# Moving the six key parts of each stacked half from the sync engine's DMA queue to POOL's own

## The chip, the cores and the metric

The kernel runs on one core of a Trainium2 chip. The metric is the time of one execution on the device, in microseconds (us); three runs of the kernel before gave 576.96 us as their median (576.51 to 578.29).

## The reference, cut to what matters

One transformer layer over x of shape (4, 512, 256), in float32: cross attention with 16 heads of 16 columns, then a mixture of experts (8 experts, top 2, plus a shared one). The change lies in the attention, where the queries come from the normalised x, the keys and values from the first 512 rows of a context (the causal mask leaves no later row), and the scores are Q K^T / 4:

```python
Q = (query @ Wq.T + bq).reshape(B, Sq, H, dk).transpose(0, 2, 1, 3)
K = (key @ Wk.T + bk).reshape(B, Sk, H, dk).transpose(0, 2, 1, 3)
scores = jnp.einsum('bhqd,bhkd->bhqk', Q, K) / jnp.sqrt(jnp.float32(dk))
scores = jnp.where(causal, scores, -jnp.inf)
attn = jax.nn.softmax(scores, axis=-1)
out = jnp.einsum('bhqk,bhkd->bhqd', attn, V)
```

## The kernel before

**Halves and stacks.** A batch of x has 512 rows and 16 heads; eight heads make a half, so there are 8 halves over the four batches. The float32 queries and keys of a half are split into three bf16 parts each (`parts`, 128 partitions by 512 columns a part). Since a head has only 16 columns, six products of parts are summed by one matmul of 96 rows: the six strips of 16 partitions of `qstack` hold the query parts in the order `Q_PART`, those of `kstack` the key parts in the order `K_PART`. Each strip is filled by one DMA that reads a part from all 128 partitions and writes 16 partitions, 1 KB a piece, 128 KB in all. So a half costs 12 such DMAs. `stack(half, u)` (L352 to L358) issues them on the sync engine SP, first the six of the queries, then the six of the keys, and all 12 count on the semaphore `rows_in[half]`.

**Who makes the parts.** TensorE (PE) projects (L643), DVE adds the bias and writes `val` (L1142), ACT rounds part 1 and part 2 (L940), and the remainders between (L502) and part 3 (L507) are POOL's in the loop, DVE's (L1149, L1154) for the first two halves. Two of the halves (u = 0 and 1) are made ahead of the loop, and each of the loop's three turns makes two more: half 0 of the next batch in the second slot, half 1 in the fourth.

**The slots.** A batch has four groups of four heads. `slot(g, ...)` on PE interleaves, by the list `SLOT`, the row maxima's scores of the next group ("R", L592 and L594, into `set_a`), the product with V of the group before ("PV", L622), and the transposed scores of this group ("S", L612, into `set_b`, which ACT's exponential L987 empties). Slots 1 and 3 begin with a projection for a coming half. The "R" matmuls of slot 3 are the first that read the new half 0, those of the next turn's slot 1 the first that read the new half 1; ahead of them stands `pe.wait_ge` on `rows_in` (L684). ACT waits for the same semaphore before it writes part 1 of the next half (L952), since the stack's DMAs read `parts`.

**The masks.** POOL sets the diagonal blocks of the exponentials to zero (L521), one call for each k of 0 to 3 in a group; `probs_v` on PE waits for `p_masked` of its k before each PV. The PVs of a group are made in the next slot: k = 0 and 1 near its start, k = 2 and 3 after "S" 7 (one row of 16 matmuls in the trace). In `mask_group` (L510 to L522) of slots 1 and 3, POOL makes part 3 between mask k = 1 and mask k = 2.

**The row maxima's rows.** `max_rows` (L361 to L364) is a DMA of 12 KB that SP issues from the same queue; the first "S" of a slot waits for it. SP works in the order of its program: in each turn `max_rows(2)`, a DMA of zeros to `x_by_slot`, `stack(0)`, `max_rows(3)`, two of zeros, `max_rows(0)`, zeros, `stack(1)`, `max_rows(1)`.

**Before the loop.** SP issues `stack(0, 0)`, `stack(1, 1)`, then `max_rows(0)`. POOL, after its constants, waits for the normalised x of all batches and adds the bias of the output to x (L489, 8.82 us).

Of the kernel before, what the change touches and what calls it, by code (L numbers as in the profile page):

```python
# [41 lines left out]
DMA = 16  # L42


def build(nc, x, ctxT, wqT, bq, wkT, bk, wvT, bv, woT, bo, gwT, wupT, wdnT, sgT, suT, sdT, out):
    B, S, D = x.shape
    H = NUM_HEADS
    DK = D // H
# [18 lines left out]
    Q_PART = (0, 0, 1, 1, 0, 2)  # L67
    K_PART = (0, 1, 0, 1, 2, 0)
# [3 lines left out]
    with ExitStack() as ctx:  # L72
# [3 lines left out]
        def sem(name):  # L76
            return ctx.enter_context(nc.semaphore(name))
# [155 lines left out]
        rows_in = [sem("rows_in0"), sem("rows_in1")]  # L233
# [4 lines left out]

        a_full, a_free, b_full, b_free = sem("a_full"), sem("a_free"), sem("b_full"), sem("b_free")
        p_masked, rc_ready, pool_turns = sem("p_masked"), sem("rc_ready"), sem("pool_turns")  # L240

        lt_full, lt_read, lg_read, logits_full, route, d_ready, ex_ready, sel_ready = (sem(n) for n in
            ("lt_full", "lt_read", "lg_read", "logits_full", "route", "d_ready", "ex_ready", "sel_ready"))
# [39 lines left out]
        B_SLOT = S_N + 1  # L283
# [43 lines left out]
        def _(sp):  # L327
# [23 lines left out]

            def stack(half, u):  # L352

                for a, (dst, order) in enumerate(((qstack, Q_PART), (kstack, K_PART))):
                    sp.wait_ge(parts_ready, 2 * u + a + 1)
                    for j, part_of in enumerate(order):
                        sp.dma_start(dst[DK * j:DK * (j + 1), half, :, :],  # L357
                                     parts[:, a, part_of, :]).then_inc(rows_in[half], DMA)  # L358

            def max_rows(g, n):  # L360
                sp.wait_ge(b_free, n + 1)  # L361
# [14 lines left out]
            def batch(b, final):  # L376
                n_b = B_ATT + b * B_PER
                if not final:

                    sp.wait_ge(a_full, A_PRO + b * A_PER - 1)  # L380
                    sp.dma_start(cV, ctxT[bass.ds(b + 1, 1)].rearrange("o (c p) n -> p (o c) n", p=P)[:, :, 0:S]
                                 ).then_inc(ld_cv, DMA)
                max_rows(2, n_b + MAX_AT)
                if not final:
                    zero_rows(4 * b + 1)
                    sp.wait_ge(b_full, n_b + B_SLOT)
                    stack(0, 2 * b + 2)
                max_rows(3, n_b + B_SLOT + MAX_AT)
                if final:
                    for w, w_dram in ((wsg, sgT), (wsu, suT), (wsd, sdT), (gw, gwT)):  # L390
                        sp.dma_start(w[:], w_dram.rearrange("(c p) n -> p c n", p=P)).then_inc(ld_moe, DMA)
                else:
                    zero_rows(4 * b + 2)
                    zero_rows(4 * b + 3)
                    max_rows(0, n_b + 2 * B_SLOT + MAX_AT)
                    zero_rows(4 * b + 4)
                    sp.wait_ge(b_full, n_b + 3 * B_SLOT)
                    stack(1, 2 * b + 3)
                    max_rows(1, n_b + 3 * B_SLOT + MAX_AT)
                    sp.dma_start(wdn[:, bass.ds(b, 1), :], wdnT[bass.ds(b * P, P)].rearrange("p (o n) -> p o n", o=1)  # L400
                                 ).then_inc(ld_moe, DMA)
# [52 lines left out]
        def _(pool):  # L454
# [29 lines left out]
            g.memset(credit[:, 0:1], 0.0).then_inc(s_yfree, 1)  # L484
            g.memset(credit[:, 1:2], 0.0).then_inc(e_yr, 1)

            pool.wait_ge(ld_o, DMA * 2)
            pool.wait_ge(xs_ready, B)
            g.tensor_tensor(xs_all[:], xs_all[:],  # L489
                            bo_bc.rearrange("p (o d) -> p o d", o=1).to_broadcast([P, T, D]),  # L490
                            ALU.add).then_inc(bo_added, 1)


            def pool_turn(signal, count):

                pool.wait_ge(signal, count)
                pool.sem_inc(pool_turns)

            def remainders(u):
                for a in range(2):  # L500
# [6 lines left out]
                    g.tensor_tensor(parts[:, a, 2, :], rem[:, a, :], parts[:, a, 1, :],  # L507
                                    ALU.subtract).then_inc(parts_ready, 1)

            def mask_group(n, last=False, split=None):  # L510

                if split is not None:
                    remainders(split)
                for k in range(QT):
                    if k == 2 and split is not None:
                        part3(split)

                    jobs = sum(job[0] <= k for job in S_JOBS)
                    pool_turn(b_free, n + jobs + (1 if jobs > MAX_AT and not last else 0))
                    diag = pT[k][:, :, 0:P]  # L520
                    g.affine_select(out=diag, in_=diag, compare_op=ALU.is_ge, fill=0.0, base=0,  # L521
                                    pattern=[[0, HG], [1, P]], channel_multiplier=-1).then_inc(p_masked, 1)  # L522

            mask_group(B_GRP0)
            with pool.Fori(0, B - 1) as b:
                for s in range(NG):
                    mask_group(B_ATT + b * B_PER + s * B_SLOT, split={0: 2 * b + 2, 2: 2 * b + 3}.get(s))
            for s in range(NG - 1):
                mask_group(B_ATT + (B - 1) * B_PER + s * B_SLOT, last=s == NG - 2)

# [42 lines left out]
        def _(pe):  # L573
# [85 lines left out]
            project_v(2, 2, 0, cT)  # L659
            pe.wait_ge(consts, 4)  # L660
            pe.wait_ge(fills, 3)
            pe.wait_ge(rows_in[0], DMA * 12)
            for j in range(A_GRP):
                rowmax_scores(0, j, 3 + j, 3 + j)
            maxima(MAX_0, B + 2, 1, first=True)
# [8 lines left out]
            def slot(g, count, n_b, par_b, rows=None, projection=None, wait_rows=None,  # L674
                     pv=True):

                at = 0
                if projection:  # L680
                    projection(*rows)
                    at = 1
                if wait_rows:
                    pe.wait_ge(*wait_rows)  # L684
                for kind, j in SLOT:
                    if kind == "R" and rows:
                        rowmax_scores((g + 1) % NG, j, rows[0] + at + j, rows[1] + at + j)
                    elif kind == "PV" and pv:
                        probs_v((g - 1) % NG, count - 1, j)
                    elif kind == "S":  # L690
                        if j == 0:
                            pe.wait_ge(max_in, DMA * (count + 1))
                        skip = 1 if rows and j >= MAX_AT else 0
                        scoresT(g, j, n_b + j + skip, par_b + j + skip)
                    elif kind == "MAX" and rows:
                        maxima(n_b + MAX_AT, par_b + MAX_AT, count + 2)
# [36 lines left out]
            def batch(b, final):  # L733
# [10 lines left out]

                for g in range(1, NG):

                    wait_rows = ((rows_in[1], DMA * 12 * (b + 1)) if g == 1 else
                                 (rows_in[0], DMA * 12 * (b + 2)) if g == 3 and not final else None)
                    projection = next_half(g // 2) if g != 2 else None
                    rows = None if final and g == 3 else (n_a, par_a)  # L750
                    slot(g, count + g, n_b, par_b, rows, projection, wait_rows)
                    if rows is not None:
                        jobs = A_GRP + (projection is not None)
                        n_a, par_a = n_a + jobs, par_a + jobs
                        n_b, par_b = n_b + 1, par_b + 1
                    n_b, par_b = n_b + S_N, par_b + S_N
# [182 lines left out]
        def _(act):  # L939
# [9 lines left out]
            def part1(u, n, w):  # L949

                if w is not None:
                    act.wait_ge(*w)  # L952
                for a in range(2):
                    act.wait_ge(*((val_ready, u + 1), (a_free, n + 1))[a])
                    copy(parts[:, a, 0, :], val[:, a, :]).then_inc(part1_ready, 1)
# [11 lines left out]
            part1(0, 0, None)  # L967
            part2(0)
            deviations(1, QT, T)
            part1(1, 1, (rows_in[0], DMA * 12))  # L970
            part2(1)

            def max_rows(n, par):
# [30 lines left out]
            def batch(b, final):  # L1004
                n, par = B_ATT + b * B_PER, B_ATT
                n_a = A_PRO + b * A_PER
                count = b * NG
                for g in range(1, NG):
                    u = None
                    if g != 2 and not final:  # L1010
                        u, job = (2 * b + 2, n_a) if g == 1 else (2 * b + 3, n_a + 2 * A_GRP + 1)

                        part1(u, job, (rows_in[1], DMA * 12 * (b + 1)) if g == 1 else
                              (rows_in[0], DMA * 12 * (b + 2)))
                    n, par = exps(n, par, (g - 1, count + g - 1), not (final and g == NG - 1), u)
                if final:
                    deviations(2, 0, T - QT)
                    p_v(NG - 1, count + NG - 1)
                    ln2_copies(0)
                    ln2_copies(1)  # L1020
                    n, par = n + 2 * C, par + 2 * C
                else:
                    n, par = exps(n, par, (NG - 1, count + NG - 1))
                for tiles in A_TILES:
                    act.wait_ge(b_full, n + 1)
                    w = len(tiles) * P
                    copy(attnT.rearrange("p c n -> p (c n)")[:, tiles[0] * P:tiles[0] * P + w],
                         bank(par)[:, 0:w]).then_inc(b_free, 1)
                    n, par = n + 1, par + 1
# [428 lines left out]
```

## Time and profile before

| what | us |
|---|---|
| median of three runs | 576.96 |
| span of the profiled execution | 575.3 |
| PE busy | 482.2 |
| DVE busy | 287.6 |
| ACT busy | 204.3 |
| POOL busy | 161.4 |
| DMA wait on the chain that ended last, `attention` to `attention` | 7.1% of the span |

The profile lists one execution with the times of each engine's instructions. The span is the time from its first to its last instruction. "SPq" and "POOLq" are instructions on an engine's own queue, DMA issues above all. A name like `attention<-attention` gives the tensor written and the tensor read; all buffers of the attention stage lie in one tensor called `attention`. In brackets at the end of a row of the timeline stands the engine's idle time ahead of it and what ended it. PEclk is the TensorE clock that was granted, as a share of 2.4 GHz; 0.50 is 1.2 GHz.

### The profile page before, as it was taken

How to read it: one execution, taken by the hardware profiler on the slowest of the kernel's cores; microseconds unless marked ns; L12 is line 12 of the kernel's file. 1: busy time of each engine (PE TensorE's matmuls, PEld its weight loads, DVE VectorE, ACT ScalarE, POOL GpSimd, SP SyncE). 2: the span in 40 equal slices, each digit the busy share in tenths (PEclk: the TensorE clock that was granted, in tenths of full speed). 3: DMA queues.
4: the chain of work that ended last, by engine and by line, in shares of the span. 5: the costliest groups of instructions: out<-in, count | busy, mean ns of one | idle time of the engine just before them, and what ended most of it. 6: DMA issues, size and time to landing. Idle time of an engine off the chain costs nothing.

```text
span 575.3 us, 9801 instructions
## 1 busy us (share of the span) xinstructions
PE 482.2 (84%) x2849; PEld 312.9 (54%) x2850; DVE 287.6 (50%) x590; ACT 204.3 (36%) x415; POOL 161.4 (28%) x186
## 2 busy tenths in 40 slices
PE   4536896999978997998879999279999999999890
PEld 2314442474424642473353555268888888888650
DVE  6746373647555572646544666114343433434357
ACT  1213464544536163544663444013232323232110
POOL 7004342312324043311211287601222222221200
PEclk9957799999979998998999999779999999999995
DMA  8759229191837539290207422212222222221168
GB/s 267 171 54 112 65 54 144 39 174 38 122 72 111 137 65 129 53 159 2 83 3 291 173 86 93 98 40 64 57 66 62 65 64 64 64 64 55 37 191 255
DMA packets 48193, 56.66 MB, mean 98 GB/s; under 512 B 10640, under 2 KB 43472, under 8 KB 47536
## 3 DMA queue, kind: packets, MB, share of 16 engines
q1 hardware_dynamic: 44768, 47.10, 38.0%
q0 software_dynamic: 3408, 9.34, 4.5%
q8 instruction: 10, 0.16, 0.1%
q14 instruction: 7, 0.06, 0.0%
HBM read 27.05 MB, written 16.59 MB: 76 GB/s over the span
## 4 chain that ended last, share of the span: by engine, by line
PE 53%; DMA 12%; DVE 9%; issue 7%; ACT 7%; POOL 6%; SPq 5%; ACTq 0%; POOLq 0%; DVEq 0%
PE set_b L889 9%; DMA attention<-attention 7%; POOL x_by_slot L555 6%; PE set_a L873 6%; PE set_a L592 5%; PE set_a L875 5%; PE set_a L874 5%; PE set_b L622 5%; SPq L357 5%; ACT attention L987 4%; PE set_a L643 3%; PE set_b L612 3%; DVE attention L1190 3%; PE set_a L798 2%; PE set_b L881 2%
## 5 line engine op out<-in xcount | busy, mean ns | idle before, releaser
L1190 DVE TENSOR_REDUCE attention<-set_a 128x2 f32<-128x1024 f32 (+2 forms) x96 | 96.7, 1042 | 57.5 <-PE set_a L594 55.6
L987 ACT ACTIVATE attention<-set_b 128x512 f32<-128x512 f32 (+1 forms) x176 | 87.5, 565 | 69.4 <-PE set_b L612 68.7
L592 PE MATMUL set_a<-attention 96*128 96x512 bf16 (+3 forms) x256 | 67.8, 330 | 32.7 <-DMA attention<-attention 26.0
L564 POOL DMA_INDIRECT y_by_choice<-moe,e_dst x39 | 37.2, 955 | 140.4 <-DVE moe L1372 131.8
L521 POOL TENSOR_SCALAR_AFFINE_SELECT attention<-attention 128x512 f32<-128x512 f32 x64 | 39.8, 634 | 116.3 <-ACT attention L987 116.2
L592 PEld LDWEIGHTS set_a<-attention 96*128 96x128 bf16 x256 | 26.7, 104 | 80.1 <-issue 46.2
L612 PE MATMUL set_b<-attention 99*128 99x512 bf16 (+3 forms) x256 | 60.8, 312 | 11.0 <-ACT attention L987 6.0
L1358 DVE TENSOR_TENSOR moe<-set_a,moe 128x384 f32<-128x384 f32 x39 | 21.7, 557 | 92.0 <-ACT moe L1075 92.0
L889 PE MATMUL set_b<-w_down,moe 128*128 x234 | 60.3, 388 | 1.1 <-DVE moe L1372 1.1
L1075 ACT ACTIVATE moe<-set_a 128x384 f32<-128x384 f32 x39 | 19.1, 490 | 116.7 <-PE set_a L875 116.7
L873 PE MATMUL set_a<-wup_hi,e_xT_hi 128*128 x156 | 57.1, 366 | 1.6 <-DVE e_xT_lo L1353 1.2
L594 PE MATMUL set_a<-maskb,identb 128*128 128x128 bf16 x256 | 53.4, 236 | 0.0
L875 PE MATMUL set_a<-wup_hi,e_xT_lo 128*128 x156 | 53.3, 341 | 0.0
L874 PE MATMUL set_a<-wup_lo,e_xT_hi 128*128 x156 | 53.1, 340 | 0.0
L622 PE MATMUL set_b<-attention 128*32 128x128 f32 (+3 forms) x512 | 47.3, 470 | 0.8 <-ACT attention L940 0.7
L889 PEld LDWEIGHTS set_b<-w_down,moe 128*128 128x128 f32 x234 | 40.0, 190 | 10.3 <-issue 7.2
L555 POOL DMA_INDIRECT x_by_slot<-moe,slots x32 | 35.1, 1098 | 28.2 <-DVE slots L1335 18.7
L643 PE MATMUL set_a<-attention 128*128 (+1 forms) x64 | 31.9, 644 | 9.0 <-DMA attention<-in_ctxT 7.8
L612 PEld LDWEIGHTS set_b<-attention 99*128 99x128 bf16 x256 | 19.6, 99 | 34.3 <-ACT attention L987 20.6
L940 ACT ACTIVATE attention<-attention 128x512 bf16<-128x512 f32 x32 | 19.3, 644 | 52.6 <-DMA attention<-attention 26.6
L873 PEld LDWEIGHTS set_a<-wup_hi,e_xT_hi 128*128 128x128 f32 x156 | 29.9, 192 | 11.1 <-issue 10.2
L940 ACT ACTIVATE attention<-set_b 12x512 bf16<-12x512 f32 (+4 forms) x48 | 25.7, 594 | 25.0 <-PE set_b L786 13.2
(152 smaller groups left out, 691.3 us busy)
## 6 DMA issues: line engine op xcount, KB each, us to landing
attention<-attention SPq DMA_DIRECT2D x96, 128.0 KB, 5.7
wup<-in_wupT SPq DMA_DIRECT2D x2, 3072.0 KB, 14.1
x_by_slot<-attention SPq DMA_DIRECT2D x13, 387.0 KB, 7.4
moe<-x_by_slot SPq DMA_DIRECT2D x39, 128.0 KB, 2.0
moe<-y_by_choice SPq DMA_DIRECT2D x16, 256.0 KB, 3.8
attention<-in_ctxT SPq DMA_DIRECT2D x7, 512.0 KB, 5.9
w_down<-in_wdnT SPq DMA_DIRECT2D x3, 1024.0 KB, 8.6
x_res<-in_x SPq DMA_DIRECT2D x4, 512.0 KB, 7.2
```

The source lines that it names most:

```text
L555: g.indirect_dma_start(xg, bass.IndirectOffsetOnAxis(slots[:, k, t:t + 1], 0), xn2[:, t, :], None).then_inc(scattered, DMA)
L592: mm(dst, qstack[0:ROWS, g // 2, h, k * P:w], kstack[0:ROWS, g // 2, h, 0:w], start=True, stop=False)
L594: last = mm(dst[:, k * P:w], identb[:], maskb[:], start=False, stop=True)
L612: last = mm(bank(par)[:, i * w:(i + 1) * w], kstack[0:ROWS + 3, g // 2, h, k * P:(k + 1) * P], qstack[0:ROWS + 3, g // 2, h, k * P:S], sta ...
L622: last = mm(pv_bank[32 * h:32 * h + 32, k * P:S], vaug[:, k, HG * g + h, :], pT[k][:, h, :], start=k == 0, stop=k == QT - 1, tile_position ...
L643: last = mm(pair(A, par)[:, a, :], w[:, c, half * P:(half + 1) * P], src[:, c, bass.ds(b * S, S)], start=c == 0, stop=c == C - 1)
L873: mm(dst, e_xT_hi[:, a, c, :], wup_hi[:, c, cols], start=c == 0, stop=False)
L874: mm(dst, e_xT_hi[:, a, c, :], wup_lo[:, c, cols], start=False, stop=False)
L875: last = mm(dst, e_xT_lo[:, a, c, :], wup_hi[:, c, cols], start=False, stop=c == C - 1)
L889: last = mm(Bk[:, 2, 0:D], e_hT[:, a, m, :], wdn[:, m, bass.ds(e * D, D)], start=m == 0, stop=m == M - 1)
L987: nc.scalar.activation(pT[k][:, h:h + heads, :], bank(par)[:, 0:heads * (S - k * P)], ACT.Exp).then_inc(b_free, 1)
L1190: v.tensor_reduce(dst, src, AX.X, ALU.max, negate=True).then_inc(a_free, 1)
```

## The change

The keys' six DMAs of a half leave SP. POOL issues them, in the same order of strips, on its own queue, and they count on new semaphores `keys_in[half]`. Where PE and ACT waited for 12 landings on `rows_in`, they wait for six on `rows_in` and six on `keys_in`. In the loop, POOL's `stack_keys` stands between part 3 and mask k = 2; it waits for `keys_read`, which SP raises once its own wait for the end of the slot's matmuls has passed. Ahead of the loop POOL issues the keys of the first two halves before it adds the output's bias.

```diff
             def stack(half, u):
-                for a, (dst, order) in enumerate(((qstack, Q_PART), (kstack, K_PART))):
-                    sp.wait_ge(parts_ready, 2 * u + a + 1)
-                    for j, part_of in enumerate(order):
-                        sp.dma_start(dst[DK * j:DK * (j + 1), half, :, :],
-                                     parts[:, a, part_of, :]).then_inc(rows_in[half], DMA)
+                sp.wait_ge(parts_ready, 2 * u + 1)
+                for j, part_of in enumerate(Q_PART):
+                    sp.dma_start(qstack[DK * j:DK * (j + 1), half, :, :],
+                                 parts[:, 0, part_of, :]).then_inc(rows_in[half], DMA)
...
                     sp.wait_ge(b_full, n_b + B_SLOT)
+                    sp.sem_inc(keys_read)
                     stack(0, 2 * b + 2)
...
                     sp.wait_ge(b_full, n_b + 3 * B_SLOT)
+                    sp.sem_inc(keys_read)
                     stack(1, 2 * b + 3)
...
+            def stack_keys(u, half):
+                pool_turn(parts_ready, 2 * u + 2)
+                for j, part_of in enumerate(K_PART):
+                    g.dma_start(kstack[DK * j:DK * (j + 1), half, :, :],
+                                parts[:, 1, part_of, :]).then_inc(keys_in[half], DMA)
+
+            stack_keys(0, 0)
+            stack_keys(1, 1)
             pool.wait_ge(ld_o, DMA * 2)
...
-            def mask_group(n, last=False, split=None):
+            def mask_group(n, last=False, split=None, half=None):
...
                     if k == 2 and split is not None:
                         part3(split)
+                        pool_turn(keys_read, split - 1)
+                        stack_keys(split, half)
...
-            pe.wait_ge(rows_in[0], DMA * 12)
+            pe.wait_ge(rows_in[0], DMA * 6)
+            pe.wait_ge(keys_in[0], DMA * 6)
...
                 if wait_rows:
-                    pe.wait_ge(*wait_rows)
+                    half, count_in = wait_rows
+                    pe.wait_ge(rows_in[half], count_in)
+                    pe.wait_ge(keys_in[half], count_in)
...
                 if w is not None:
-                    act.wait_ge(*w)
+                    half, count_in = w
+                    act.wait_ge(rows_in[half], count_in)
+                    act.wait_ge(keys_in[half], count_in)
```

## Rows read from the trace of the kernel before

**Rows 1.** The page: the chain that ended last, by engine.
```profile
PE 53%; DMA 12%; DVE 9%; issue 7%; ACT 7%; POOL 6%; SPq 5%; ACTq 0%; POOLq 0%; DVEq 0%
```

**Rows 2.** Waits: engine, line, releaser: us in total, times, longest.
```profile
ACT attention L940 <- DMA attention<-attention: 26.6, 4, 8.1
PE set_a L592 <- DMA attention<-attention: 26.0, 4, 13.6
```

**Rows 3.** Timeline of PE: start, us, instruction, idle before.
```profile
36.97 0.59 PE L592 MATMUL set_a<-attention 96*128 96x512 bf16 x1 [13.55 <-DMA attention<-attention]
...
59.13 0.61 PE L612 MATMUL set_b<-attention 99*128 99x512 bf16 x1 [2.69 <-DMA attention<-attention]
...
98.30 0.47 PE L592 MATMUL set_a<-attention 96*128 96x512 bf16 x1 [4.17 <-DMA attention<-attention]
```

**Rows 4.** Timeline of SP's queue: start, us, instruction.
```profile
21.72 30.13 SPq L357 DMA_DIRECT2D attention<-attention  x24
51.89 0.86 SPq L363 DMA_DIRECT2D attention<-attention  x1
...
83.04 7.80 SPq L357 DMA_DIRECT2D attention<-attention  x12
...
112.40 8.46 SPq L357 DMA_DIRECT2D attention<-attention  x12
```

**Rows 5.** The issues of L357: ns each min/median/max, and landings.
```profile
L357 SPq DMA_DIRECT2D attention<-attention x96: 547/607/1326, 21.7 to 248.3; - x96
...
DMA to landing us min/median/max: 3.2/5.7/8.1
```

**Rows 6.** Timeline ahead of the loop: DVE's part 3, ACT's copy of the maxima's rows.
```profile
21.00 1.35 DVE L1154 TENSOR_TENSOR attention<-attention 128x512 bf16<-128x512 f32 x2
...
47.98 0.59 ACT L940 ACTIVATE attention<-set_b 12x512 bf16<-12x512 f32 x1 [5.52 <-PE set_b L602]
```

**Rows 7.** Windows: length, busy by engine, PEclk, DMA share, GB/s.
```profile
30.00:34.00 4.00, 0.00 (x0) 0.00 (x0) 0.37 (x2) 0.00 (x0) 0.00 (x0) 0.50 1.14 119
...
90.00:94.00 4.00, 3.95 (x14) 1.63 (x12) 0.00 (x0) 2.08 (x5) 1.56 (x3) 1.00 1.14 121
128.00:130.00 2.00, 2.00 (x11) 1.77 (x10) 0.42 (x1) 0.00 (x0) 0.00 (x0) 1.00 0.97 390
...
57.50:64.30 6.80, 5.17 (x26) 3.28 (x27) 2.70 (x4) 2.28 (x4) 3.03 (x2) 0.50 0.26 58
...
98.50:101.90 3.40, 3.40 (x15) 0.85 (x14) 1.23 (x1) 0.93 (x2) 2.26 (x2) 0.50 0.36 107
```

**Rows 8.** The chain in order of time: start, us, what.
```profile
28.92 7.80 DMA attention<-attention
...
90.23 7.95 DMA attention<-attention
```

**Rows 9.** Timeline of POOL, masks and part 3 of the loop's first turn.
```profile
79.69 2.27 POOL L507 TENSOR_TENSOR attention<-attention 128x512 bf16<-128x512 f32 x2
81.96 1.22 POOL L521 TENSOR_SCALAR_AFFINE_SELECT attention<-attention 128x512 f32<-128x512 f32 x2
```

**Rows 10.** Timeline of PE: the PVs of k = 2 and 3, the projection.
```profile
88.37 0.86 PE L622 MATMUL set_b<-attention 128*32 128x256 f32 x16
...
90.48 3.65 PE L643 MATMUL set_a<-attention 128*128 x8
...
117.79 0.86 PE L622 MATMUL set_b<-attention 128*32 128x256 f32 x16
```

**Rows 11.** Timeline of POOL: its indirect DMAs of the routing stage.
```profile
332.85 0.96 POOL L555 DMA_INDIRECT x_by_slot<-moe,slots  x1 [0.30 <-issue]
334.11 2.41 POOL L555 DMA_INDIRECT x_by_slot<-moe,slots  x1 [0.30 <-issue]
336.82 1.36 POOL L555 DMA_INDIRECT x_by_slot<-moe,slots  x1 [0.30 <-issue]
```

**Rows 12.** Timeline of DVE, beside those DMAs.
```profile
333.94 6.75 DVE L1348 TENSOR_TENSOR wup_lo<-wup,wup_hi 128x1536 fp32r<-128x1536 f32 x4
```

More of the change, by code:

```diff
@@ L240, in build @@
         p_masked, rc_ready, pool_turns = sem("p_masked"), sem("rc_ready"), sem("pool_turns")
+        keys_read = sem("keys_read")
+        keys_in = [sem("keys_in0"), sem("keys_in1")]
         lt_full, lt_read, lg_read, logits_full, route, d_ready, ex_ready, sel_ready = (sem(n) for n in
@@ L485, in _, with pool_turn @@
             g.memset(credit[:, 1:2], 0.0).then_inc(e_yr, 1)
+            def pool_turn(signal, count):
+                pool.wait_ge(signal, count)
+                pool.sem_inc(pool_turns)
+            def stack_keys(u, half):
[5 more added lines that the diff above has]
+            stack_keys(1, 1)
             pool.wait_ge(ld_o, DMA * 2)
@@ L491, in _ @@
                             ALU.add).then_inc(bo_added, 1)
-            def pool_turn(signal, count):
-                pool.wait_ge(signal, count)
-                pool.sem_inc(pool_turns)
             def remainders(u):
@@ L526, in _ @@
                 for s in range(NG):
-                    mask_group(B_ATT + b * B_PER + s * B_SLOT, split={0: 2 * b + 2, 2: 2 * b + 3}.get(s))
+                    mask_group(B_ATT + b * B_PER + s * B_SLOT, split={0: 2 * b + 2, 2: 2 * b + 3}.get(s),
+                               half={0: 0, 2: 1}.get(s))
             for s in range(NG - 1):
@@ L745, in batch @@
                 for g in range(1, NG):
-                    wait_rows = ((rows_in[1], DMA * 12 * (b + 1)) if g == 1 else
-                                 (rows_in[0], DMA * 12 * (b + 2)) if g == 3 and not final else None)
+                    wait_rows = ((1, DMA * 6 * (b + 1)) if g == 1 else
+                                 (0, DMA * 6 * (b + 2)) if g == 3 and not final else None)
                     projection = next_half(g // 2) if g != 2 else None
@@ L969, in _ @@
             deviations(1, QT, T)
-            part1(1, 1, (rows_in[0], DMA * 12))
+            part1(1, 1, (0, DMA * 6))
             part2(1)
@@ L1011, in batch @@
                         u, job = (2 * b + 2, n_a) if g == 1 else (2 * b + 3, n_a + 2 * A_GRP + 1)
-                        part1(u, job, (rows_in[1], DMA * 12 * (b + 1)) if g == 1 else
-                              (rows_in[0], DMA * 12 * (b + 2)))
+                        part1(u, job, (1, DMA * 6 * (b + 1)) if g == 1 else
+                              (0, DMA * 6 * (b + 2)))
                     n, par = exps(n, par, (g - 1, count + g - 1), not (final and g == NG - 1), u)
```

## The prediction, made before the changed kernel was run

> **What bounds the kernel now.** Read the page first: PE is busy for 482.2 of 575.3 us, and it has 53% of the chain that ended last, but DMA has 12% of it and SP's queue 5% [rows 1]. So not all of the time is PE's work. The waits name the DMAs: ACT and PE stood for 26 us each for transfers within `attention`, four times each [rows 2]; those are the stacks. The timeline of PE places them: 13.55 us ahead of the first "R", then 4.17 us at the "R" of slot 3 in the loop's first turn, and 4.20 and 4.06 us at the same place of the other two turns; beside these, 2.69 us ahead of the first "S" [rows 3]. The first four have the stack's landing as their end, the fifth the landing of `max_rows(0)`, which SP issued right behind 24 DMAs of two stacks [rows 4]. The chain goes the same way: last DMA of a stack issued at 28.92 and at 90.23, landed 7.8 and 7.95 us later [rows 8].
>
> Next comes why the rows land late, since that decides everything. SP issues 12 in 7.80 us, 0.65 us each [rows 4]. A DMA needs at the least 3.2 us from issue to landing, but the median is 5.7 [rows 5]: they queue. While they do, the queues are busy throughout (share 1.14) and move 119 to 121 GB/s [rows 7], so 131,072 bytes take 1.09 us, more than SP's 0.65 us. Twelve take 13.1 us. SP's issue is not what limits the stack; the movement of the data is. Yet the same 16 engines at a share of 0.97 move 390 GB/s when 2 KB pieces go to all partitions [rows 7]. What differs is that a stack's DMA writes 16 partitions only. Two DMAs in flight to different strips could thus go faster than two to one strip.
>
> **The change, part by part.** Six issues leave SP, 3.9 us a half; nothing on the chain waits for SP's own time but `max_rows(0)`. The new semaphores and waits of PE and ACT add an instruction each on queues that stand idle or run ahead there; I count nothing for them (a wait that is already met costs below 0.1 us, and even 20 of them on the path would be 2 us, which the range holds). What counts is two prices: how fast the rows land when two queues feed the engines, and what six issues cost POOL.
>
> *POOL's pace p.* No row of before shows a direct DMA from POOL. Below stands SP's pace for the same DMA, 0.65 us [rows 4]. The nearest row is POOL's indirect DMA, also 128 pieces of 1 KB: 0.96 us busy and 0.30 us to the next, a pace of 1.27 [rows 11]. Above stand the ones beside DVE's L1348, which reads two SBUF tensors: 1.36 busy, so 1.67, and one of 2.41 [rows 11, 12]. In the loop DVE mostly reduces out of `set_a` meanwhile, so I don't take the stretched ones. A direct DMA reads no list of indices, so I go a little under the nearest row: p = 1.2, of which 0.9 busy.
>
> *Landing.* I take it that the two queues mix: SP runs ahead by a strip at once (0.65 against 1.2 us), so that mostly two different strips are being written. The last key DMA then lands 3.2 us after its issue. It costs nothing if so, 0 to 5 us at each stop if not (the rival below).
>
> *Ahead of the loop.* Key part 3 is ready at 21.00 + 1.35 = 22.35 [rows 6], POOL is idle. Last key DMA issued 22.4 + 5p = 28.4, landed 31.6, in place of 36.7 [rows 8]: 5.1 us. In general 36.7 - 25.6 - 5p = 11.1 - 5p. The 2.69 us ahead of the first "S" go too: ACT's copy ends at 48.57 [rows 6], 43.5 when all is 5.1 earlier; SP is then through with its six (the second stack's twelve issues end at 51.85 [rows 4] and so began at 44.1; 44.1 - 5.1 + 3.9 = 42.9), so `max_rows(0)` goes out behind 6 stack DMAs and not 12, at 43.5, and PE asks for it at 56.4 - 5.1 = 51.3, 7.8 us later, as long as it needed before. Sum: 13.8 - 5p = 7.8 us. POOL's bias addition may start up to a microsecond later behind the keys of u = 1; nothing on the chain waits for it.
>
> *In the loop, slot 3.* POOL's part 3 ends at 81.96, then it waits with SP for `keys_read`; SP's stack starts at 83.04 [rows 4, 9]. Behind the six issues on POOL stand mask k = 2 and k = 3, which ran at 81.96 to 83.18 before. Issues end 6p - 0.3 = 6.9 later, mask k = 2 takes 0.63: 90.57. PE wants that PV at 88.37 [rows 10], and mask k = 3 costs it 0.17 more. So a new stop s = 6p - 0.3 + 0.63 + 0.17 - 5.33 = 6p - 4.83 = 2.4 us. This was hidden by 5.2 us of cover before, and now that is used up. PE reaches the "R" of slot 3 at 94.13 + 2.4 = 96.5. The keys land at 83.0 + 6.0 + 3.2 = 92.2, so no wait is left there: the mean stop of 4.1 us becomes 2.4.
>
> *Slot 4 (slot 0 of the next batch).* The same six issues come for half 1 at 112.40, the PV is wanted at 117.79, 5.39 later [rows 4, 10]: again 2.4 us. Here nothing is won: the rows are first read in the next turn's slot 1, behind the end of the batch. ACT and PE have no slack left by which to catch up after a PV, for the transposes of the output wait on it.
>
> *The clock.* After each 4.1 us stop PE ran at a granted clock of 0.50 for 3.4 us or more [rows 7]; at 1.2 GHz in place of 2.4 that is 1.7 us a turn. The stop of 2.69 us was followed by 0.50 too, 57.5 to 64.3. Two stops of 2.4 us in a turn in place of one of 4.1 may leave one such stretch, none or two. I take one: no change, with 1.7 us a turn to both sides.
>
> *Sum.* Ahead of the loop 13.8 - 5p, in the loop 3 (4.1 - 2s) = 3 (13.8 - 12p), together 55 - 41p: each 0.1 us of POOL's pace is worth 4 us. With p = 1.2 that is 7.8 - 2.0 = 5.8, rounded to 6 us faster. The profiled span is 575.3 us, so 569.3, and the median of the runs stands 1.7 us above it: 571.
>
> The Trainium skill, "SBUF — State Buffer", section "Door 1: The DMA port swizzle", says that partitions reach the DMA side over 16 ports, picked by bits of the partition number, so that a strip of 16 partitions has four. An estimate by its 27 GB/s a port is 109 GB/s for a strip, near the 119 to 121 measured, and by it two strips at a time would reach about twice that. By that rule the sum above stands.
>
> **The rivals.** *The data still bind.* The rows land as late as before whoever issues them: 120 GB/s, 13.1 us for twelve. For it speaks that the queues are at 1.14 already and SP has 5 us of lead; if POOL's j-th DMA moves in step with SP's j-th, both write one strip. Against it: 390 GB/s in another pattern. Then nothing is won ahead of the loop and in slot 3, where the 2.4 us are hidden before the unchanged 98.3, and slot 4 pays 3 x 2.4 = 7.1 us: 584 us. It decides where the twelve take D: x = 13.1 - D is won once ahead of the loop and in each of three turns, 4x against 7.1, so from x below 1.8, D above 11.3 us. The Trainium skill, "DMA: Bandwidth & Descriptors", section "Issuing engines are not separate DMA queues", says that issuing from several engines saves only the time on the sequencer; no run here has tested it yet, and by it this is the case that comes.
>
> *POOL's issues are dear.* At p = 1.5 the masks come 4.2 us late in two places of each turn: 13.8 - 7.5 = 6.3 won ahead, 3 (4.1 - 8.3) = -12.7 in the loop, 583 us. It turns slower from p = 1.34 on. The row of 1.27 lies near, those of 1.67 beyond.
>
> *POOL's issues are cheap.* At p = 0.95, s is 0.9: 9.1 + 3 (4.1 - 1.7) = 16 us, and stops of 0.9 us should leave the clock up, 3 x 1.7 = 5 more: 556 us. For it speaks the lack of indices; against it that both kinds write as many pieces.
>
> *It doesn't do what it says:* the new stop in slot 3 is as long as the old and the rows were never last. The named releaser of four stops speaks against that.
>
> **How the numbers follow.** The forecast 0.45 (p from 1.05 to 1.34, 565 to 577 us), data bind 0.22, dear issues 0.13, cheap issues 0.15, the rest 0.05. By the bounds of p: at 0.65 no stop is left, 10.5 + 12.3 + 5.1 gives 549; at 1.67, 5.4 - 18.6 gives 590. Leaving out the outer ends of the cheap and dear cases, 559 to 585. What can be told from no change here is 0.3%, 1.7 us. Faster: 0.38 of the forecast's share, the cheap case and a little of the rest, 0.56; same 0.10; slower 0.34.
>
> **What would show it.** POOL's issues in the profile: pace 1.2, six in 7 us. PE's first "R" near 31.8 in place of 36.97 and no wait for a DMA ahead of the first "S". In the loop, no DMA wait at L592, but two stops of about 2.4 us a turn at L622, released by POOL L521. During the stacks, well over 120 GB/s. The prediction is wrong if L592 still waits for `attention<-attention` in the loop, or if the PVs of k = 2 don't wait for the masks, or wait for over 4 us.

## The result, and the profile after

The changed kernel takes 582.11 us (median; 581.51 to 583.16) against 576.74 us of the kernel before: a ratio of 1.0085, 95% interval 1.0063 to 1.0108. It is 5.4 us slower; 6 us faster was forecast. The profiled execution has a span of 580.4 us against 575.3.

Waits of the changed kernel, which answer to [rows 2]:

```profile
ACT attention L957 <- DMA attention<-attention: 28.0, 4, 8.3
PE set_a L606 <- DMA attention<-attention: 27.4, 4, 13.8
```

None of the stops that were to go has gone. The timeline of PE, against [rows 3], says so at each place:

```profile
37.24 0.59 PE L606 MATMUL set_a<-attention 96*128 96x512 bf16 x1 [13.77 <-DMA attention<-attention]
...
59.87 0.61 PE L626 MATMUL set_b<-attention 99*128 99x512 bf16 x1 [3.17 <-DMA attention<-attention]
...
99.50 0.61 PE L606 MATMUL set_a<-attention 96*128 96x512 bf16 x1 [4.95 <-DMA attention<-attention]
```

The stops are 13.77, 3.17 and 4.95 us where they were 13.55, 2.69 and 4.17. The POOL rows, which answer to [rows 9], show what I had feared, the masks behind POOL's issues:

```profile
80.41 2.28 POOL L518 TENSOR_TENSOR attention<-attention 128x512 bf16<-128x512 f32 x2 [0.27 <-ACT attention L957]
84.07 3.14 POOL L499 DMA_DIRECT2D attention<-attention  x6 [1.39 <-SPq L388]
87.22 1.81 POOL L534 TENSOR_SCALAR_AFFINE_SELECT attention<-attention 128x512 f32<-128x512 f32 x3
```

POOL issues six DMAs in 3.14 us, a pace of 0.52 us, less than SP's 0.65 [rows 4] and less than half of the 1.2 that I took. The masks of k = 2 and 3 are through in time and the PV is not stopped:

```profile
88.79 0.64 PE L636 MATMUL set_b<-attention 128*32 128x256 f32 x8
```

Now the data. First come the window 90 to 94 us, the same as in [rows 7], and the stretch behind the stop (length, busy by engine, PEclk, DMA share, GB/s). Then follow the chain, and the landings of SP's and of POOL's stack DMAs:

```profile
90.00:94.00 4.00, 3.95 (x18) 1.84 (x16) 0.00 (x0) 2.49 (x5) 1.63 (x3) 1.00 1.05 108
98.50:105.20 6.70, 5.70 (x25) 1.23 (x26) 2.45 (x2) 1.15 (x2) 2.27 (x2) 0.50 0.37 107
```
```profile
87.00 12.38 DMA attention<-attention
```
```profile
L358 SPq DMA_DIRECT2D attention<-attention x48: 547/613/2298, 21.8 to 248.1; - x48
...
DMA to landing us min/median/max: 3.3/8.2/12.4
```
```profile
L499 POOL DMA_DIRECT2D attention<-attention x48: 530/530/760, 23.1 to 247.4; - x48
...
DMA to landing us min/median/max: 4.2/8.1/12.5
```

With two queues 108 GB/s are moved where one queue moved 121. The last of the twelve goes out at 87.00 us, 3.2 us before that of the old kernel (90.23 [rows 8]), and all that they do is wait longer: a median of 8.2 us to landing and not 5.7 [rows 5]. The last to land is that last query DMA of SP, 12.38 us after its issue. From the first issue to the last landing a stack takes 15.8 us in the first turn's slot 3, 15.4 and 15.0 in the others, where it took 15.1, 15.1 and 15.0, and 16.4 against 15.1 for the second stack ahead of the loop. The granted clock after the stop of 4.95 us is 0.50 for 6.7 us and not for 3.4 [rows 7].

By place: at the same matmul after the loop, which waits for DVE in all kernels, the changed kernel stands 3.1 us behind. The kernel before, then the changed one:

```profile
263.51 0.34 PE L592 MATMUL set_a<-attention 96*128 96x384 bf16 x1 [1.12 <-DVE attention L1190]
```
```profile
266.61 0.34 PE L606 MATMUL set_a<-attention 96*128 96x384 bf16 x1 [1.12 <-DVE attention L1209]
```

The span ends 5.1 us behind. So 2 us are lost after the attention, where the change touches nothing. The routing stage's indirect DMAs on POOL, which answer to [rows 11], before and then after:

```profile
L555 POOL DMA_INDIRECT x_by_slot<-moe,slots x32: 956/960/2406, 326.4 to 370.0; - x32
```
```profile
L569 POOL DMA_INDIRECT x_by_slot<-moe,slots x32: 965/969/2522, 329.0 to 373.9; - x32
```

From the start of the first to the end of the last they take 45.94 us against 44.59, which is 1.35 of the 2 us. The rest comes behind them, where kernels differ by as much without the change: from the end of these DMAs to the end of the span pass 205.5 us here and 204.3 before, and 204.2 to 205.4 in the five other kernels below in which POOL issues no direct DMA.

### The profile page after: what moved, and what is told of

The parts are those of the page before. It is cut to its first block, busy times and chain, and to the rows that moved or that the text cites. A ratio compares the mean times of both kernels' runs of the same rounds, so it can differ in the third digit from the quotient of the medians.

```text
span 580.4 us, 9830 instructions
## 1 busy us (share of the span) xinstructions
PE 484.7 (84%) x2849; PEld 312.4 (54%) x2850; DVE 288.0 (50%) x590; ACT 204.2 (35%) x415; POOL 188.5 (32%) x234
## 4 chain that ended last, share of the span: by engine, by line
PE 53%; DMA 16%; DVE 9%; POOL 7%; issue 6%; ACT 6%; SPq 3%; ACTq 0%; POOLq 0%; DVEq 0%
DMA attention<-attention 10%; PE set_b L906 9%; POOL x_by_slot L569 6%; PE set_a L890 6%; PE set_b L636 5%; PE set_a L606 5%; PE set_a L892 5%; PE set_a L891 5%; ACT attention L1006 4%; PE set_a L657 3%; DVE attention L1209 3%; PE set_a L815 2%; PE set_b L626 2%; DMA moe<-y_by_choice 2%; PE set_b L898 2%
## 5 line engine op out<-in xcount | busy, mean ns | idle before, releaser
L636 PE MATMUL set_b<-attention 128*32 128x128 f32 (+3 forms) x512 | 50.8, 501 | 0.4 <-ACT attention L957 0.3
L569 POOL DMA_INDIRECT x_by_slot<-moe,slots x32 | 36.5, 1140 | 28.2 <-DVE slots L1354 18.7
L499 POOL DMA_DIRECT2D attention<-attention x48 | 25.6, 541 | 39.4 <-DVE attention L1173 29.8
```

The source lines that it names most:

```text
L569: g.indirect_dma_start(xg, bass.IndirectOffsetOnAxis(slots[:, k, t:t + 1], 0), xn2[:, t, :], None).then_inc(scattered, DMA)
L636: last = mm(pv_bank[32 * h:32 * h + 32, k * P:S], vaug[:, k, HG * g + h, :], pT[k][:, h, :], start=k == 0, stop=k == QT - 1, tile_position ...
```

## The experiments

Theory A says that the write into 16 neighbouring partitions binds a stack's DMAs, theory B that an engine moves such pieces at that rate wherever they go. The rows of a stack may stand in any order, so long as queries and keys have the same; that makes A easy to test. The kernel before, spread:

```diff
-                        sp.dma_start(dst[DK * j:DK * (j + 1), half, :, :],
+                        sp.dma_start(dst[j:ROWS:6, half, :, :],
```

> The kernel before, with the 96 rows of the stacks laid out otherwise: part j of column d goes to partition 6d + j in place of 16j + d, for queries and keys alike, so that the sums are the same and each DMA writes 16 partitions that lie 6 apart. Theory A (the write into 16 neighbouring partitions binds a stack at 1.09 us a DMA): the twelve run at SP's pace of 0.65 us, the rows land near 32 us in place of 36.7 ahead of the loop, the stops of 4.1 us in the loop go with their stretches of half clock, 5.8 us a turn; 552 us. Theory B (an engine moves pieces from SBUF to SBUF at about 7.5 GB/s whatever they write): nothing changes, 577 us.

Measured: 548.80 us, ratio 0.9501 (0.9473 to 0.9529), and once more 548.50, 0.9499 (0.9477 to 0.9522). Its repetition had this expectation:

> The spread kernel before once more, on the chip of the kernel with ACT's six DMAs, to compare the two: 549 us, as the first time.

The waits, the window of a stack in the second turn, and the landings of the spread kernel:

```profile
PE set_a L592 <- DMA attention<-attention: 8.7, 1, 8.7
...
ACT attention L940 <- DMA attention<-attention: 3.2, 1, 3.2
```
```profile
134.00:140.00 6.00, 5.58 (x56) 3.13 (x55) 4.26 (x8) 4.86 (x11) 1.27 (x2) 1.00 0.75 208
```
```profile
DMA to landing us min/median/max: 2.3/2.4/3.7
```

The three stops in the loop and that ahead of the first "S" are gone; the one ahead of the first "R" is left, with 8.7 us. The queues move 208 GB/s at a share of 0.75, and no DMA waits for another: 2.4 us from issue to landing is the median as well as nearly the least. Theory A holds and B falls: only the place of the 16 partitions was changed. Here SP's issue is what binds.

The changed kernel in the same layout (`qstack[j:ROWS:6, ...]` on SP, `kstack[j:ROWS:6, ...]` on POOL):

> The changed kernel with the same layout of rows, partition 6d + j. Theory A: with the write unbound, the two queues' issues count (SP 0.65, POOL 0.52 us each, side by side), rows land near 29 us ahead of the loop, some 3 us before those of the kernel before in this layout; in the loop both are early enough; 549 to 552 us. Theory B: 582 us, as the changed kernel.

Measured: 550.58 us, 0.9533 (0.9509 to 0.9557). The stop ahead of the first "R" is 8.06 in place of 8.66 us, and that is all that the second queue gains: the last of the twelve is issued 4.2 us after the first, where SP by itself needs 7.2, but they still land 0.65 us apart. In the profiles it stands 0.4 us behind the spread kernel on one queue after the loop and 3.8 at the end, so again the loss comes after the attention: 1.4 us of it are in the 32 indirect DMAs (45.98 against 44.59). The medians are 1.8 us apart.

The keys' strips from the last to the first in the changed kernel:

```diff
-                for j, part_of in enumerate(K_PART):
+                for j, part_of in reversed(list(enumerate(K_PART))):
```

> The changed kernel; POOL issues the keys' strips from the sixth to the first while SP goes from the first to the sixth, so the two queues write different strips nearly always. If the two queues of the changed kernel only met in the same strip, this frees them: over 150 GB/s during a stack, rows 3 us or more earlier, 570 us or less. If all 16 engines take their turns between the queues in step, so that they are all in one strip at any time whatever the order, or if theory B holds: about 120 GB/s and 582 us.

Measured: 576.58 us, 0.996 (0.993 to 0.999), midway between the two forecasts. Waits and first "R" of slot 3:

```profile
PE set_a L606 <- DMA attention<-attention: 25.0, 4, 13.5
```
```profile
97.13 0.41 PE L606 MATMUL set_a<-attention 96*128 96x512 bf16 x1 [3.87 <-DMA attention<-attention]
```

From first issue to last landing a stack of slot 3 takes 14.6 to 14.8 us, where the old kernel took 15.0 to 15.1 and the changed one 15.0 to 15.8. The matmul after the loop is at 262.09 us, 4.5 us ahead of the changed kernel and 1.4 ahead of the old one (0.4 us of that stood already when its first stack was issued). Only the order of the strips differs from the changed kernel, and the two intervals of the ratio (0.993 to 0.999, 1.0063 to 1.0108) lie apart, so the order costs the changed kernel time. The reading is that its two queues meet in the same strip: POOL's first issue comes 0.5 us behind SP's, and its fifth is ahead of SP's fifth. But two strips at once don't give twice the rate; a stack is through 2 to 3% sooner than with one queue.

The packets of the traces show more. POOL's are of 4 KB and SP's of 1 KB, so they can be told apart, and their order gives the strip. Of the time in which both queues have a packet under way, both write the same strip for 37% in the changed kernel and for 5% in this one. And of the time in which both have a stack to write, one queue holds 90% or more of the packets under way for 40% here: with some 16 packets under way at a time, the engines swing together from one queue to the other. But while neither holds over 70% (23% of the time), the packets move at 139 GB/s, and at 124 while one holds nearly all. So even side by side, two strips are not written at twice the rate.

All twelve on POOL (the query loop moved into `stack_keys`):

> The changed kernel with all twelve DMAs of a half issued by POOL, queries then keys, on its one queue. If it is the alternation between two queues that makes the stack of the changed kernel last 14.5 us and not 13.7: first packet to last landing is back near 13.5 us, the stops at the first row maxima of slot 3 are 4.2 us, and what is added are the masks behind six more issues (3.1 us), a stop of 1 to 2 us before the PV of k = 2 in slots 3 and 4: 579 to 584 us. If it is POOL's descriptors themselves (4 KB packets): the twelve take 15 us or more, and the time is over 585 us.

Measured: 581.46 us, 1.0068 (1.0046 to 1.0091). The twelve take 14.7 to 14.8 us from first issue to last landing in the loop (15.4 in one stack of six; the old kernel 15.0 to 15.3), so POOL's descriptors are no slower than SP's. The masks behind twelve issues:

```profile
87.82 1.01 PE L636 MATMUL set_b<-attention 128*32 128x256 f32 x16 [2.21 <-POOL attention L534]
```
```profile
80.83 3.15 POOL L496 DMA_DIRECT2D attention<-attention  x6 [1.70 <-SPq L385]
83.97 3.15 POOL L499 DMA_DIRECT2D attention<-attention  x6
87.12 2.39 POOL L534 TENSOR_SCALAR_AFFINE_SELECT attention<-attention 128x512 f32<-128x512 f32 x4
```

This is the stop that the prediction had put into the changed kernel, at 12 x 0.52 in place of 6 x 1.2: issues end at 87.12, a mask takes 0.63, PE goes on at 87.82. It comes at all six places, with 2.1 to 2.2 us each. PE wanted the PV at 85.61, 4.8 us after POOL's first issue and not the 5.33 of the prediction; six issues at 0.52 us fit under either.

Two layouts between neighbours and stride 6. The kernel before at stride 3:

```diff
+                        sp.dma_start(dst[48 * (j // 3) + j % 3:48 * (j // 3) + 48:3, half, :, :],
```

> The kernel before with each DMA of a stack writing 16 partitions that lie 3 apart (part j of column d at 48 (j // 3) + j % 3 + 3d). If the 16 partitions' sharing of ports binds, by the port table of the Trainium skill up to three of them are on one port, against four neighbouring ones at stride 1 and two at stride 6: 3/4 of 1.09, 0.82 us a DMA, so the twelve land 12.0 us after the first issue and not 15.1; the stops of 4.1 us in the loop shrink to about 1, time near 560 us. If only direct neighbours bind, it is as fast as stride 6, 0.65 us a DMA and 549 us.

And the changed kernel at stride 2 (`32 * (j // 2) + j % 2 : 32 * (j // 2) + 32 : 2` for both stacks):

> The changed kernel with each DMA of a stack writing 16 partitions that lie 2 apart, two to a port in all six strips. With stride 6 the two queues' twelve took 0.65 us a DMA, though both were issued by 3.7 us; by the port rule stride 2 should do 0.55 to 0.65 us as well, the loop without stops, 549 to 552 us. If nearness and not the port counts: between stride 1 and stride 6, 0.8 us or more a DMA and 560 us or more.

Measured: stride 3, 551.24 us, 0.9554 (0.9524 to 0.9583); stride 2 on two queues, 550.56 us, 0.9548 (0.9526 to 0.9571). Windows of stacks, stride 3 and then stride 2:

```profile
136.00:144.00 8.00, 7.59 (x59) 3.98 (x58) 4.01 (x8) 6.09 (x13) 2.40 (x4) 1.00 1.04 189
```
```profile
77.00:83.00 6.00, 5.75 (x46) 2.89 (x45) 2.55 (x6) 5.10 (x11) 3.46 (x7) 1.00 0.99 180
```

Stride 3 takes about 0.7 us a DMA, 10.5 to 11.5 us from first issue to last landing in the loop where 12.0 was expected: better than that estimate, worse than stride 6. The share of 1.04 at 189 GB/s, against 0.75 at 208, says that the queues are busy throughout again; that is little over SP's own pace, and a DMA lands 3.5 us after its issue and not 2.4. Neighbours are the worst by far, and any spreading takes most of the gain; the exact law is not settled by four layouts.

What loses time after the attention? Three kernels ask this. First, the keys of the first two halves alone on POOL, ahead of the loop:

```diff
+            for u in range(2):
+                pool.wait_ge(parts_ready, 2 * u + 2)
+                for j, part_of in enumerate(K_PART):
+                    g.dma_start(kstack[DK * j:DK * (j + 1), u, :, :],
+                                parts[:, 1, part_of, :]).then_inc(keys_in[u], DMA)
```

> The kernel before, with the keys of the first two halves alone issued by POOL (ahead of the loop), all of the loop's by SP. All four kernels with direct DMAs on POOL so far spent 45.94 to 45.98 us in the 32 indirect DMAs of the routing stage, where before and the spread kernel before spent 44.59, and 1 us more in the last results. Theory P (having issued direct DMAs at all slows POOL's later ones): 45.9 us here too, indirect DMAs of 0.97 us in place of 0.96, and a time some 2 us above before, 579. Theory L (the 36 direct DMAs of the loop, or what changed with them, do it): 44.6 us and 577.

Measured: 580.32 us, 1.005 (1.003 to 1.007), the 32 indirect DMAs in 45.97 us. But its profile (581.7 us, the slowest of six runs) also stands 3.6 us behind the old kernel at the matmul after the loop, though all stacks of the loop go out on SP alone. Then the semaphores, three of them that nobody uses, which shift the numbers of all later ones:

```diff
+        unused = [sem("unused0"), sem("unused1"), sem("unused2")]
```

> The kernel before with three semaphores allocated that nobody uses, so that all later ones have the numbers that they have in the changed kernel. Theory P: nothing, 44.6 us in the routing stage's DMAs, 577 us. Theory S (the slower end is a matter of which semaphores the indirect DMAs count on): 45.9 us and 579 us.

Measured: 578.45 us, 1.0019 (0.9997 to 1.0041), the 32 in 44.58 us. Theory S falls. This kernel does the same work as the one before, and so it shows what a single profile is worth. Its first stop of the loop is as long as before, but the half clock behind it lasts for 6.6 us and more, where the old kernel had it for 3.4 [rows 7]:

```profile
97.22 0.60 PE L593 MATMUL set_a<-attention 96*128 96x512 bf16 x1 [4.15 <-DMA attention<-attention]
```
```profile
96.80:103.40 6.60, 6.18 (x27) 1.53 (x28) 2.45 (x2) 1.15 (x2) 2.27 (x2) 0.50 0.24 71
```

From its first stack's issue to the matmul after the loop it takes 243.6 us, and the old kernel 241.8. Last, one load of 1 KB (bq) issued by POOL as its first work, on a semaphore of its own:

```diff
-            sp.dma_start(bqc, bq).then_inc(ld_q, DMA)
...
+            g.dma_start(bqc, bq).then_inc(ld_bq, DMA)
```

> The kernel before with one 1 KB load (bq) issued by POOL at its very start, on a semaphore of its own, and no other direct DMA on POOL. Theory P1 (one direct DMA is enough to slow POOL's indirect ones later): 45.9 us in the routing stage's 32 indirect DMAs, 0.97 us each, time near 579. Theory P2 (it takes many, or large ones): 44.6 us, 577.

Measured: 580.46 us, 1.0042 (1.0025 to 1.0059), the 32 in 45.96 us. POOL's groups, of this kernel, of the one with three semaphores, and of the changed one (busy us, mean ns, idle before):

```profile
L565 POOL DMA_INDIRECT y_by_choice<-moe,e_dst x39 | 37.8, 968 | 139.4 <-DVE moe L1374 130.8 <-DVE e_dst L1371 6.3 <-DMA y_by_choice<-moe,e_dst 2.3
L556 POOL DMA_INDIRECT x_by_slot<-moe,slots x32 | 36.5, 1141 | 28.2 <-DVE slots L1337 18.7 <-issue 9.5
...
L456 POOL DMA_DIRECT2D attention<-in_bq x1 | 0.7, 722 | 0.8 <-POOLq L1453 0.8
```
```profile
L565 POOL DMA_INDIRECT y_by_choice<-moe,e_dst x39 | 37.2, 955 | 139.5 <-DVE moe L1373 130.9 <-DVE e_dst L1370 6.3 <-DMA y_by_choice<-moe,e_dst 2.3
L556 POOL DMA_INDIRECT x_by_slot<-moe,slots x32 | 35.1, 1098 | 28.2 <-DVE slots L1336 18.8 <-issue 9.4
```
```profile
L569 POOL DMA_INDIRECT x_by_slot<-moe,slots x32 | 36.5, 1140 | 28.2 <-DVE slots L1354 18.7 <-issue 9.4
```

One direct DMA of 1 KB, 325 us earlier, is enough for the slower indirect ones. Each indirect DMA takes 0.01 us more, which is 0.3 us over the 32; about 1.1 us come on top, since a second one of them is now held for 2.5 us where DVE's second run of four L1348 begins, as in all kernels with this shift. Together that is 1.4 us in the trace. That the one brings about the other was not tried by itself. By the runs the whole costs 2.4 us (0.42% of 577.6; 1.4 to 3.4 by the interval), so some 1 us is not located; what in POOL brings it about stays open.

The last version uses a second queue without POOL: the spread kernel with the key DMAs of the very first half on ACT:

```diff
+            act.wait_ge(parts_ready, 2)
+            for j, part_of in enumerate(K_PART):
+                act.dma_start(kstack[j:ROWS:6, 0, :, :], parts[:, 1, part_of, :]).then_inc(keys_0, DMA)
```

> The kernel before with the rows at partition 6d + j (as the spread kernel before), and the six key DMAs of the very first half issued by ACT, which stands idle there from 22 us on; all others stay with SP. In that layout SP's pace of 0.65 us is what the twelve take. Theory A: two queues now halve the issue and nothing else binds before about 0.65 us a DMA at the data (what two queues reached with POOL), so the first rows land 0 to 1 us earlier than in the spread kernel: 548 to 549 us, no difference that can be told. If the 0.65 us with two queues came from POOL's packets: rows at 29.7 in place of 32.5, 546 us.

Measured: 549.24 us, 0.9505 (0.9477 to 0.9532), on the same chip as the spread kernel's 548.50: no difference that can be told. The first stop is 8.19 us and not 8.52. Nothing here is faster than the spread kernel on SP's single queue, 29 us faster than the one before.

## Why the prediction was wrong, point by point

**What bounds the kernel.** Right: the five stops and their releaser, the 1.09 us a DMA, and the reading that the writing of 16 neighbouring partitions limits it and not SP's issue. The spread layout confirms this, and it moved the time by 5%.

**Landing.** This is the step that failed: "I take it that the two queues mix", with SP ahead by a strip, "so that mostly two different strips are being written. The last key DMA then lands 3.2 us after its issue." POOL's pace of 0.52 us let it catch up with SP, and the two were in one strip for 37% of the time. But that isn't the heart of it: with the strips apart at almost all times (keys reversed) a stack still took 14.6 to 14.8 us in place of 15.0 to 15.1. I had taken the limit of a strip for one that a second strip stands outside of, and the estimate that two strips reach about twice the rate of one did not hold: over a stack (86 to 97 or 98 us) 136 GB/s were moved with the keys reversed and 116 in the changed kernel, where the one queue had moved 131. So the last DMA of the first turn's stack landed 12.4 us after its issue and not 3.2, and neither the 7.8 us ahead of the loop nor the mean stop of 4.1 us in each turn could be won. Nor did it help `max_rows(0)` to stand behind six DMAs of SP and not twelve: it went out at 48.85 us and not at 51.89, and the first "S" still stood for 3.17 us. Why two strips share one rate stays open. The engines do take turns together between the queues, but they gain little also while they don't (139 against 124 GB/s), so this alone is not the reason, and no trace here tells one engine's packets from another's.

**POOL's pace.** Mis-sized: 1.2 us forecast, 0.52 measured. The nearest row, POOL's indirect DMA of 0.96 + 0.30 us, was no guide to a direct one, which follows on its predecessor with no gap. With 0.52 the formula 6p - 4.83 is below nothing, and no PV was stopped. The prediction's rivals of dear and cheap issues were both worked out with a pace above 0.9, and the lower bound, 0.65 with 549 us, still took the landing for granted. The 7.1 us of stops that I had counted for the case that the data bind were never paid: its 584 us lie close to the 582 measured, but for a wrong reason. The mechanism is real: with twelve issues the stop comes, 2.2 us.

**The rival "the data still bind".** Right in its mechanism and wrong in its price. It said that nothing is won in the rows' landing, and so it was. What it didn't have are the two things that cost the time. The first is 3.1 us in the attention by the two profiles: the five stops are longer by 1.9 us in sum, and the first turn has a longer stretch of half clock, worth up to 1.7. The second is 1.35 us in POOL's slower indirect DMAs (with one tiny DMA on POOL the runs differ by 2.4 us in all); what is lost behind them, 0.7 us, is not tied to anything. Of the first part, the strips' order decides the most by the runs: with the keys reversed the ratio is 0.996 and not 1.0085. But the split of a single profile isn't sharp. The kernel with three unused semaphores has the longer half clock too, and takes 1.8 us more than the old one over the same stretch; the one whose loop is SP's alone stands 3.6 us behind. What the Trainium skill says in "DMA: Bandwidth & Descriptors", "Issuing engines are not separate DMA queues", that a second engine saves sequencer time only, was borne out: in the old layout the last issue came 3.2 us sooner and the rows landed no sooner, and in the spread one, where issue does bind, the second queue won 0.6 us ahead of the loop.

**The clock.** I left it at no change. Behind the first turn's stop the stretch at 0.50 was 6.7 us and not 3.4, but this can't be laid to the stop's 4.95 us: the semaphore kernel had as much behind 4.15 us, and the old kernel 6.8 us behind the 4.20 and 4.06 of its own second and third turns. The guess on shorter stops can be answered from the kernel with all twelve on POOL: its two mask stops of 2.1 to 2.2 us a turn were each followed by 3.4 us at half clock, so two such stops cost as much clock as one of 4.1 followed by 6.8, and more than one followed by 3.4.

## What to carry to other kernels

Before issuing DMAs from a second queue, look at the share of the DMA queues during the burst: if it is at 1 while few bytes move, as here (1.14 at 121 GB/s), the data bind and not the issue. Another issuer did not help here; changing what each DMA writes did. The copies from SBUF into 16 neighbouring partitions ran at a third of what the queues moved in a load to all partitions (121 against 390 GB/s), and where the row order is free, a stride between the partitions costs nothing. And a layout is cheaper to test than a queue: one slice was worth 29 us here.

## What the runs showed of the hardware that I had not expected

- Twelve copies of 128 KB from 128 partitions into 16 of stride 1, 3 and 6 land about 1.09, 0.7 and 0.65 us apart on one queue (the last is SP's pace of issue). On two queues, stride 2 gives 180 GB/s and stride 6 gives 210.
- Two queues that write different strips of neighbours at the same time move 139 GB/s by the packets under way, where one at a time moves 124; that is far from twice as much.
- A direct DMA of 128 pieces of 1 KB costs POOL 0.53 us, with no gap to the next; an indirect one of as many pieces 0.96 and a gap of 0.30.
- After a single direct DMA on POOL, its indirect DMAs take 0.969 to 0.972 us in the routing stage in place of 0.960 to 0.963, in all seven kernels that had one and in none of the six that had none; the 32 take 45.9 to 46.0 us in place of 44.6.
